# A first attention whose first pair's maxima are taken during the context projection, with its keys fetched there and the values copied by ScalarE

## What is computed

```python
q = (query @ Wq + bq).reshape(B, Nq, H, D).transpose(0, 2, 1, 3)
k = (key_value @ Wk + bk).reshape(B, Nkv, H, D).transpose(0, 2, 1, 3)
v = (key_value @ Wv + bv).reshape(B, Nkv, H, D).transpose(0, 2, 1, 3)
attn = jnp.einsum('bhqd,bhkd->bhqk', q, k) * scale
attn = jnp.clip(attn, -CLAMP, CLAMP)
attn = jax.nn.softmax(attn, axis=-1)
...
x = jnp.einsum('bhqk,bhkd->bqhd', attn, v).reshape(B, Nq, Cq)
return x @ Wo + bo
```

## Time and profile before

| | |
|---|---|
| median of three runs | 1168.22 us |
| the profiled execution | 1164.9 us |
| its span | 1163.7 us |
| keys phase, to the barrier's end | 0 to 141.0 us |
| heads phase before its first exponential | 141.0 to 172.5 us |
| heads phase, first to last exponential | 172.5 to about 515 us |
| busy over the span | TensorE 83%, VectorE 71%, ScalarE 54%, GpSimd 22% |

### The profile page before, as it was taken

How to read it: one execution, slowest core, us unless ns; L and a number is a source line. 1 busy time by engine, 2 the same in 40 slices (tenths; PEclk the granted TensorE clock), 3 DMA queues, 4 the chain that set the end, 5 groups by cost and what they waited for, 6 DMA issues and landing times. The chain is left out here.

```text
span 1163.7 us, 20413 instructions
## 1 busy us (share of the span) xinstructions
PE 969.7 (83%) x7503; PEld 589.6 (51%) x7520; DVE 829.5 (71%) x1753; ACT 627.7 (54%) x1018; POOL 258.4 (22%) x281
## 2 busy tenths in 40 slices
PE   6997769999999999985879998518878878996586
PEld 5886624444444444443765565314455555744354
DVE  5775688999999999913542447998888786256447
ACT  3443317887887888872331114139999998202121
POOL 1000188899300000000000002003554632000010
PEclk9999959999999999997769998558799998997797
DMA  5867632223223223102011216302164226740000
GB/s 179 312 226 256 254 113 73 74 79 83 73 77 86 73 75 86 44 1 57 1 55 62 85 44 181 96 0 60 38 173 133 69 80 213 176 137 1 0 1 19
DMA packets 99319, 111.80 MB, mean 96 GB/s; under 512 B 26658, under 2 KB 75730, under 8 KB 99218
## 3 DMA queue, kind: packets, MB, share of 16 engines
q1 hardware_dynamic: 96802, 109.50, 31.2%
q10 hardware_dynamic: 2416, 0.99, 0.4%
HBM read 80.95 MB, written 29.43 MB: 95 GB/s over the span
## 5 line engine op out<-in xcount | busy, mean ns | idle before, releaser
L835 ACT ACTIVATE pT<-bank 128x512 f32<-128x512 f32 x512 | 278.4, 597 | 93.5 <-PE bank L752 72.2
L857 DVE TENSOR_REDUCE rmax<-bank 128x2 f32<-128x1024 f32 x256 | 307.3, 1223 | 26.5 <-PE bank L720 25.7
L764 PE MATMUL bank<-pT,V 128*17 128x256 f32 x2048 | 161.1, 387 | 4.7 <-ACT oT L841 4.6
L1600 PE MATMUL bank<-K1s,qs 97*128 97x512 f32 x256 | 116.1, 555 | 58.6 <-ACT below L1709 37.2
L752 PEld LDWEIGHTS bank<-qs,ks 49*128 49x128 f32 x1024 | 77.8, 187 | 112.4 <-ACT pT L835 98.9
L752 PE MATMUL bank<-qs,ks 49*128 49x256 f32 x1024 | 130.0, 332 | 2.3 <-ACT pT L835 0.5
L1864 POOL TENSOR_TENSOR total<-total,work 128x1024 f32<-128x1024 f32 x40 | 94.9, 2380 | 154.7 <-ACT work L1718 153.9
L720 PE MATMUL bank<-ks,qs 49*128 49x512 f32 x512 | 110.6, 427 | 16.4 <-DMA ks<-k_parts_d 9.2
L1600 PEld LDWEIGHTS bank<-K1s,qs 97*128 97x128 f32 x256 | 54.0, 224 | 73.9 <-ACT below L1709 38.6
L1770 DVE MAX8 cand<-work 128x8 f32<-128x128 f32 x384 | 76.5, 280 | 0.0
L764 PEld LDWEIGHTS bank<-pT,V 128*17 128x17 f32 x2048 | 34.6, 95 | 63.0 <-ACT pT L835 43.6
(11 more groups left out here) (442 smaller groups left out, 1789.5 us busy)
## 6 DMA issues: line engine op xcount, KB each, us to landing
k_parts_d<-kparts SPq DMA_DIRECT2D x48, 512.0 KB, 3.6
ks<-k_parts_d SPq DMA_DIRECT2D x381, 64.0 KB, 2.2
K1s<-k_parts_d SPq DMA_DIRECT2D x96, 128.0 KB
cn<-in_ctx SPq DMA_DIRECT2D x32, 384.0 KB, 3.6
cx<-in_ctx SPq DMA_DIRECT2D x16, 384.0 KB
w<-in_L_ffn_w SPq DMA_DIRECT2D x32, 128.0 KB
w2e<-in_L_ffn_w SPq DMA_DIRECT2D x16, 128.0 KB
W<-in_L_xattn_W SPq DMA_DIRECT2D x2, 1024.0 KB, 9.6
```

Of the source, the lines that this page charges most:

```text
L764: t = pe.matmul(bank[32 * c:32 * c + VW, 7, a * S:(a + 1) * S], V[:, b * NCH + 4 * g + c, h, :], pT[:, (at + 2 * (c // 2) + a) % 8, c % 2 ...
L835: p_made.up(act.activation(pT[:, at % 8, :], bank[:, 4 + at % 3, :], ACT.Exp))
L857: max_read.up(dve.tensor_reduce(rmax[p % 2][:, :, qt, c], bank[:, b0:b0 + 2, :], AX.X, ALU.max))
L1600: m = pe.matmul(bank[:, b0 + c, :], qs1[0:NROW1, b * H1 + h, q], K1s[h][0:NROW1, keys], start=True, stop=(what == "new"))
```

## The change

The 16 maxima steps of pair 0 leave the heads phase. They become 32 units in the keys phase, one head and 512 keys each: a matmul into bank 7 (`first_scores`) and a VectorE maximum over 512 columns (`first_maximum`). Six units a block stand at blocks 10 to 14 and two at block 15: one behind each key tile, and one behind each of the last three value quarters. As there is one bank, unit u waits until unit u - 1 is read. After block 15 the 16 maxima are transposed and written into the query row. Pair 0's and pair 1's keys get tiles of their own (`kf`), fetched by ScalarE's queue in the keys phase; ScalarE issues 36 more transfers there. ScalarE copies the values into `V` without bias (two copies a block), and GpSimd adds the bias in place. SyncE no longer stores the queries. The s4 steps move to earlier blocks, and the exponential's table is loaded at block 1. In the heads phase the main loop starts at once; 21 maxima steps of pairs 1 and 2 are spread over the 16 j of pair 0. GpSimd's powers wait until pairs 0 and 1 are scored, as they lie where `kf` lies.

```diff
+    kf = [sb(f"kf{j}", [P, S2], F32R) for j in range(2)]
...
+    FIRST_FROM, FIRST_SLOTS = 10, 6
...
-            if n in (8, 9):
-                store_queries(n - 8)
...
     def store_queries(mt):
-        sp.wait_ge(*q_split.at(2 * mt + 2))
+        act.wait_ge(*q_split.at(2 * mt + 2))
...
-                q_stored.up(sp.dma_start(q_stack_d[h0:h0 + P // D0, r0:r0 + D0, :], qparts[:, mt, qp, b * S:(b + 1) * S].bitcast(F32)), 16)
+                q_stored.up(act.dma_start(q_stack_d[h0:h0 + P // D0, r0:r0 + D0, :], qparts[:, mt, qp, b * S:(b + 1) * S].bitcast(F32)), 16)
...
+    def load_first_keys(p, k):
+
+        for j in range(2):
+            act.wait_ge(*kparts_out[j].at(48 * 2 * (k + 1)))
+        cols = slice(k * S2 // 2, (k + 1) * S2 // 2)
+        for a in range(2):
+            for r0, kp, qp in STACK:
+                kf_in[p][k].up(act.dma_start(kf[p][HALF_P * a + r0:HALF_P * a + r0 + D0, cols].bitcast(F32),
+                                             k_parts_d[(2 * p + a) * D0:(2 * p + a + 1) * D0, kp, cols]), 16)
...
+                act.preload_act_table_set("natural_log_exp_and_others")
...
-            if n in (11, 12):
+            if n in (8, 9):
                 next(s4, None)
+            for h in range(2):
+                act.wait_ge(*v_made.at(2 * n + h + 1))
+                c0 = n * 4 + 2 * h
+                v_copied.up(act.copy(V[:, c0:c0 + 2, :, 0:D0], bank[:, 5 + h, :].rearrange("p (c h d) -> p c h d", c=2, h=H0)))
+            if n in (2, 3):
+                act.wait_ge(*ones_made.at(1))
+                key_ones(act, kf[n - 2], kf_in[n - 2])
+            if n in (5, 6):
+                load_first_keys(n - 5, 0)
+            if n == 7:
+                store_queries(0)
+            if n == 8:
+                act.wait_ge(*q_stored.at(16 * (1 + 2 * NSTK)))
+                for pair in range(2):
+                    load_queries(act, pair)
+            if n == 9:
+                load_first_keys(0, 1)
+            if n == 10:
+                store_queries(1)
+            if n == 11:
+                load_first_keys(1, 1)
...
+        for n in range(NBLK):
+            for h in range(2):
+                c0 = n * 4 + 2 * h
+                pool.wait_ge(*v_copied.at(2 * n + h + 1))
+                v_biased.up(pool.tensor_tensor(V[:, c0:c0 + 2, :, 0:D0], V[:, c0:c0 + 2, :, 0:D0],
...
+        def first_maximum(n, slot):
+            u = FIRST_SLOTS * (n - FIRST_FROM) + slot
+            if 0 <= u < 32:
+                dve.wait_ge(*first_made.at(u + 1))
+                first_read.up(dve.tensor_reduce(rmax[0][:, u % 2, u // 2 % 2, u // 4:u // 4 + 1], bank[:, 7, :], AX.X, ALU.max))
...
+                first_maximum(n, m)
+            for slot in range(3, FIRST_SLOTS):
+                first_maximum(n, slot)
...
-            if n in (8, 9, 10, 11, 13):
+            if n in (2, 3, 4, 5, 10):
                 next(s4, None)
+        first_queries()
...
+            if u == 0:
+                pe.wait_ge(*s4T_made.at(6))
+                pe.wait_ge(*query_in[0].at(32))
+            else:
+                pe.wait_ge(*first_read.at(u))
...
     def ahead(p, j):
+        if p == 0:
+            n = 16 + LEAD
+            return [what for at in range(j * n // 16, (j + 1) * n // 16) for what in steps_of(1 + at // 16, at % 16)]
...
+        pool.wait_ge(*st_made.at(2 * UNITS))
...
-        for at in range(place[1, LEAD - 1] + 1):
-            pass_on(*passing[at])
...
```

More of the change, by code:

```diff
@@ L300, in build @@
     V = sb("V", [P, NB * NCH, H0, VW])
+    HALF_P = P // 2
+    rmax = [sb(f"rmax{j}", [P, 2, 2, 8]) for j in range(2)]
+    fold = sb("fold", [P, VW])
+    below = spot[0]
+    spot[0] = LATER + 2 * 4 * LB * 32 * 4
+    qs = [sb(f"qs{j}", [P, S], F32R) for j in range(3)]
+    nmax = sb("nmax", [P, 2, P])
+    kf = [sb(f"kf{j}", [P, S2], F32R) for j in range(2)]
+    assert spot[0] <= END
+    spot[0] = below
+    kf_in = [[flag(f"kf_in{j}{k}") for k in range(2)] for j in range(2)]
+    query_in = [flag(f"query_in{j}") for j in range(3)]
+    fold_made, nmax_zeroed = flag("fold_made"), flag("nmax_zeroed")
+    first_made, first_read, first_max, first_turned, first_rows = (flag(n) for n in (
+        "first_made", "first_read", "first_max", "first_turned", "first_rows"))
+    FIRST_FROM, FIRST_SLOTS = 10, 6
     phase_begins()
@@ L506, in queries, with first_scores @@
             q_made.up(t)
+        def first_scores(n, slot):
+            u = FIRST_SLOTS * (n - FIRST_FROM) + slot
+            if not 0 <= u < 32:
+                return
+            a, qt, c = u % 2, u // 2 % 2, u // 4
+            rows = slice(HALF_P * a, HALF_P * a + NROW)
+            if u == 0:
[3 more added lines that the diff above has]
+                pe.wait_ge(*first_read.at(u))
+            if u % 16 == 0:
+                pe.wait_ge(*kf_in[0][u // 16].at(16 * 8))
+            first_made.up(pe.matmul(bank[:, 7, :], qs[0][rows, qt * P:(qt + 1) * P], kf[0][rows, c * 512:(c + 1) * 512],
+                                    start=True, stop=True))
         pe.wait_ge(*ident_made.at(1))
@@ L537, in keys_tensor @@
                 queries(n - 5)
-            if n in (11, 12):
+            if n in (8, 9):
+                if n == 8:
+                    pe.wait_ge(*q_taken.at(2))
                 next(s4, None)
+        pe.wait_ge(*first_max.at(1))
+        for qt in range(2):
+            t = pe.transpose(bank[:, 7, qt * P:(qt + 1) * P], nmax[:, qt, :], ident[:, :])
+        first_turned.up(t)
     run(keys_sync, keys_vector, keys_scalar, keys_pool, keys_tensor)
     phase_ends()
-    NP_, HALF_P = NH // 2, P // 2
+    NP_ = NH // 2
     G = 8
@@ L577, in steps_of @@
     def steps_of(m, u):
-        return [(m, u)] + [(m - 1, "rows")] * (u == 0 and m > 0)
+        return [(m, u)] + [(m - 1, "rows")] * (u == 0 and m > 1)
     def ahead(p, j):
+        if p == 0:
+            n = 16 + LEAD
+            return [what for at in range(j * n // 16, (j + 1) * n // 16) for what in steps_of(1 + at // 16, at % 16)]
         m, u = p + 1 + (j + LEAD) // 16, (j + LEAD) % 16
@@ L585, in beside, with keys_of @@
         return ahead(p, j) + [(p - 1, "sums")] * (j == 4 and p > 0)
-    passing = [what for u in range(16) for what in steps_of(0, u)]
-    passing += [what for u in range(LEAD) for what in steps_of(1, u)]
-    for p in range(NP_):
-        for j in range(16):
-            passing += beside(p, j)
-    passing += [(NP_ - 1, "sums")]
+    passing = [what for p in range(NP_) for j in range(16) for what in beside(p, j)] + [(NP_ - 1, "sums")]
     place = {what: at for at, what in enumerate(passing)}
+    def keys_of(p):
+        return kf[p] if p < 2 else ks[p % 2]
     def powers_pool():
@@ L720, in max_step @@
                 t = pe.matmul(bank[:, 2 * (at % 2) + a, :], qs[p % 3][rows, qt * P:(qt + 1) * P],
[L721 removed]
+                              keys_of(p)[rows, c * 512:(c + 1) * 512], start=True, stop=True)
             max_made.up(t)
@@ L751, in scores @@
                     rows = slice(HALF_P * a, HALF_P * a + NROW)
-                    t = pe.matmul(bank[:, 4 + (at + a) % 3, c * S:(c + 1) * S], ks[p % 2][rows, k0:k0 + P],
+                    t = pe.matmul(bank[:, 4 + (at + a) % 3, c * S:(c + 1) * S], keys_of(p)[rows, k0:k0 + P],
                                   qs[p % 3][rows, :], start=True, stop=True)
```

111 lines of the change are left out of this document (56 added, 55 removed).

## The result

The changed kernel takes 1184.18 us (median of 8 runs, 1176.6 to 1191.34) against 1168.78 for the kernel before in the same session: ratio 1.0126, 95% interval [1.0085, 1.0167]. It is slower by a little over 1%. The forecast was 1172.0, with a range of 1149 to 1188. The kernel before was run again beside the experiments: its median is 1168.58 beside experiments 1 to 4, 1170.07 beside 5 to 8, 1170.59 beside 9 to 12, and 1170.04 over all 94 executions. Now and then an execution is slower as a whole; the ratios leave these out, the medians of experiments 1, 2, 3, 6 and 9 count one each.

A forecast was written before the change was run, and what follows sets the result against it. VectorE's maxima were taken to bound the heads, with TensorE busiest in the keys phase. Heads -21.8, blocks 5 to 9 -2.4, blocks 10 to 14 +24.5, end +2, clock +4.8: +7.1 on 1164.9 gives 1172.0 us, range 1149 to 1188.

The forecast's parts named there:

- the likeliest case: Whole kernel: the forecast itself, 1172.0 us, alone spanning 1163 to 1179, chance 0.45.
- The sum: Whole kernel: -21.8 - 2.4 + 24.5 + 2 + 4.8 = +7.1 us on the profiled 1164.9.
- the slower rival: Blocks 10 to 14: TensorE's clock falls in block 10 and stays low, 16.5 us a block, 1184.6 total; chance 0.18.
- Blocks 5 to 9: Keys phase: context in time with SyncE free of query stores, 39.5 us in place of 41.9, gain 2.4.
- the prices: ScalarE's issue time in the keys phase: 2.8 us for six key loads, 4.7 for six query stores.
- the rival on transfers: Blocks 6 to 9: early key fetches make the context late, two stalls of 3.7 us, 1179 total; chance 0.08.
- Blocks 10 to 14: Keys phase with six units a block: 65.1 us in place of 40.6, a loss of 24.5.
- The chain behind ScalarE: Blocks 10 to 14: each maximum waits behind `kl` and ScalarE's cast, stopping TensorE; 10.7 us a block without issues.
- the lower bound of 8.0: Blocks 13 and 14: at least TensorE's 6.6 us plus six units at 0.22.
- The clock in blocks 10 to 12: One gap of 3.5 to 5 us a block lowers TensorE's clock for 3.2 us: 3 x 1.6 = +4.8 us.
- The heads: Pair 0's loop ends 31.9 us behind the barrier in place of 53.7, set by VectorE's maxima: gain 21.8 us.
- GpSimd's additions: Keys phase: 32 bias additions, at most 2.4 us per two value copies, ending about 1.3 us behind the last copy.

The follow-up runs named there:

- experiment 1: Changed kernel with the four one-row fills of the later pairs' key tiles issued by SyncE, not ScalarE: 1186.3 us, ratio 1.0126 to the kernel before.
- experiment 2: Changed kernel with ScalarE's keys-phase issues moved ahead of the same block's two value copies: 1178.76 us, ratio 1.0094 to the kernel before.
- experiment 3: Changed kernel without pair 0's 32 maxima units, a constant standing in for the maxima: 1154.25 us, ratio 0.984 to the kernel before.
- experiment 4: Changed kernel with values moved and biased by VectorE again, no ScalarE copies or GpSimd additions: 1177.33 us, ratio 1.0059 to the kernel before.
- experiment 5: Changed kernel, blocks 10 to 15: maxima ahead of key low parts, next context's low parts behind the last: 1176.2 us, ratio 1.0051.
- experiment 6: As experiment 2, with later key loads and stores and GpSimd writing pairs 0 and 1's one-rows: 1178.91 us, ratio 1.0064 to the kernel before.
- experiment 7: Changed kernel with experiment 5 and experiment 6 combined: 1181.19 us, ratio 1.0099 to the kernel before.
- experiment 8: Changed kernel with four unread filler matmuls while TensorE waits for the first exponential: 1180.4 us, ratio 1.0106 to the kernel before.
- experiment 9: Changed kernel with pair 0's maxima back ahead of the heads, all else kept: 1170.08 us, ratio 0.9996 to the kernel before.
- experiment 10: Kernel before with 24 early key loads added on ScalarE in blocks 5, 6, 9 and 11, read by nobody: 1173.48 us, ratio 1.0037.
- experiment 11: Kernel before with its twelve query stores issued by ScalarE, two a block in blocks 7 to 12: 1161.29 us, ratio 0.9932.
- experiment 12: Changed kernel with experiment 9, experiment 4, experiment 11's stores, only pair 0's keys early, three loads a block: 1161.95 us, ratio 0.9939 to kernel before.

## Why the prediction was right and wrong

**Within its range, at its slow end.** 1184.2 lies in 1149 to 1188, in the part that the prediction had left for slower (0.23), and outside the likeliest case's own 1163 to 1179. The sum was +7.1; in the same session the medians differ by 1184.18 - 1168.78 = 15.4, so 8.3 of the 12.2 us of the miss are the sum's. The other 3.9 are the base: the profiled execution of 1164.9, that the sum was put on, lies that far under the median. The prediction knew of 3.3 and left them out. That the measured time is within 0.4 us of the slower rival's 1184.6 is chance: that rival did not happen as told.

**Blocks 5 to 9: the step that failed.** Forecast 39.5, a gain of 2.4; measured 48.5 from cast to cast, a loss of 6.6, and 44.2 by TensorE's transposes, a loss of 2.4. Two sentences carry the forecast. "SyncE is free of the query stores, so the context comes in time" is wrong: TensorE waits for it 1.65 and 2.67 us in these blocks, and its clock is at 0.50 for some 3 us behind the second wait (0.78 over block 8). Those 4.3 us are nearly all that TensorE's 44.2 has over the forecast. "ScalarE then finishes up to 2 us late, but nothing waits for it within a block" is half right: beside the context TensorE waited only 0.55 us there, for a query tile, but at block 10 it was 5.5 - 1.1 = 4.4 us late, and there TensorE waits 4.93 us for the maximum. The groups took 3.81, 5.12, 7.40, 2.42 and about 5.1 us where the prices were 2.8 and 4.7, and stood at the end of the block behind the value copies.

How long an issue takes is not what fills these blocks. Six kernels have the same program for them (the kernel after and experiments 1, 3, 5, 8 and 9, but for a memset in 3). Their six stores took 7.40, 4.67, 3.90, 8.92, 4.83 and 6.24 us to issue; the blocks took 48.0 to 49.6 us from cast to cast and 43.7 to 44.9 by TensorE's transposes: 5 us more of issue moved them by 1.5 us at most. Experiments 2 and 4, without the issues ahead of the casts or without the copies, have 44.3 and 43.6. What they share is a context that is late. Experiment 11 has 38.7 us, and experiment 10 has loads without stores at no cost. So the rival on transfers, at 0.08, had the place right. Against it stood 0.77 MB beside 1.9 MB, a sum of bytes; but the share of the transfers' time alone doesn't settle it either, as 0.92 was free in experiment 10. What went up is the time from the context's issue to its use, 5.2 us before, 9.8 after. Why it takes so long stays open, the more since the share is 0.46 in the last 2.7 us of that wait. Blocks 0 to 4 lost 2.5 us that the prediction had at nothing; the eight one-row fills on ScalarE lie in them (4.13 us for the first four), and no experiment took them out alone.

**Blocks 10 to 14: the total right, its terms wrong.** Blocks 10 to 13 were forecast at 15.1 + 15.1 + 13.5 + 10.7 = 54.4, with 4.8 of clock, and took 56.6 (18.1, 15.6, 11.4, 11.5); the stretch from the cast of block 14 to the barrier was to grow by 6.1 and grew by 6.2. By TensorE's transposes, where ScalarE's lag falls into block 10, they are 157.26 - 96.36 = 60.9. Experiment 3 puts the 32 units at 32.8 us. The chain behind ScalarE is real in blocks 10 and 11, where experiment 5 takes 9.6 us out of it. In block 10 it is as told: the second unit starts 8.9 us behind the first transpose (105.28 - 96.36). But in block 13 it isn't what sets 11.4 us: there experiment 5 changes nothing, since TensorE itself pays 6 x 0.66 = 4 us for its units, and 6.6 + 4.0 = 10.6; it is busy 10.59 of 11.40 us there, VectorE 7.44, and the rest are waits of 0.56 and 0.23 us for a maximum. The chain of 10.7 us and TensorE's own work happened to be equal, and the lower bound of 8.0, from 0.22 us a unit, was far too low. A unit put between runs of other matmuls costs three times its columns; which of its differences does it (another row count, other weights, a bank of its own) is not separated.

**The clock in blocks 10 to 12: another term that was too small.** It did not stay low from block to block, as the rival had it: PEclk is 0.74 on the mean of these blocks and 1.00 in block 13. But each fall lasted far longer than the 3.2 us taken: 0.50 from about 105 to 118, behind the wait of 4.93 us, and from about 125 to 135, behind one of 2.05, while TensorE was busy without a gap. (1 - 0.74) x 45.1 is 11.7 us of the engine at full rate, against 1.6 before (0.94 over 27.4 us): 10 more, where 4.8 were forecast. The three blocks still took 45.1 us, and 43.7 + 4.8 = 48.5 was forecast. So what was not clock took about 33 us where 43.7 were forecast: the chain was priced too high, the clock too low, and the total owes its fit in part to luck.

**The heads: the count right, the clock not.** 21.8 us were forecast. At a granted clock of 0.94 (experiment 1) the time from barrier to first `oT` copy is better than forecast; at 0.50 it is 43.3 us against 34.3 forecast (31.9 and four exponentials), 9.0 lost. The prediction had looked at the lower clock and found it harmless, with 2.2 us more TensorE work against 6.1 on VectorE; but at 0.50 TensorE is busy 38.4 of 40.2 us. A step of pair 0 then takes 2.1 to 2.6 us where VectorE needs 21 / 16 x 1.22 = 1.6. In nine executions of kernels with this first pair, the time from first exponential to first `oT` copy was 28.1, 30.7, 31.5, 32.6, 33.5, 38.6, 38.6, 40.4 and 40.4 us; 30.4 was forecast. The mean, 34.9, makes the gain near 17 us, and experiments 3 and 9 put it at 14 to 18. TensorE: Matmul & The Clock Gate, section HAM oscillation, in the Trainium skill tells of loops that fall back to the lower clock when TensorE waits in them; the trace of this kernel shows also the other thing, a TensorE busy 96% of 40 us that stayed at 0.50. The four kernels whose TensorE had stood longest for the first exponential had the lowest clock (experiment 8), but that the wait is the cause is not shown: experiment 1 has hardly such a wait (0.42 us), and four of its six executions took 1185 us or more, at a mean granted clock of 0.870 to 0.878 against 0.894 of the other two.

**The other steps.** First exponential 3 to 4 us behind the barrier: 2.9. GpSimd's additions: 1.2 us each, hidden. Later pairs nearly unchanged: 244.84 - 222.21 = 22.6, then 22.0.

## What to carry to other kernels

Before transfers are moved into a stage, neither their bytes nor the share of the transfers' time says whether there is room: a share of 0.92 was free in one place, and 5 us were lost in another. Look for the transfer that the critical engine waits for next, what stands ahead of it on its queue, and how long it takes from issue to use (5.2 us before, 9.8 after). Don't give an issue one price: the same six stores, in the same place of the same program, took 3.9 to 8.9 us; ask what stands behind them, and whether anything waits for that. Count a stage on the engine that sets it: by ScalarE's casts these five blocks lost 6.6 us, by TensorE's transposes 2.4. Taking a burst of stores off the queue that the context is issued on, and spreading it, two a block, gave 9 us in the median with nothing else moved. And where a new matmul is put between others, take its price from a row of such a change of shape; if there is none, its columns are a lower bound only.
